# Cross-attention on one core: value and denominator products joined, reciprocals on query lanes, row maxima started two steps earlier

## The reference

```python
def _L0_xattn_ref(target, source, target_mask, source_mask, Wq, bq, Wk, bk, Wv, bv):
    ...
    dot = jnp.einsum('bhdt,bhds->bhts', q, k) / math.sqrt(HEAD_DIM)
    mask = target_mask[:, :, :, None] * source_mask[:, :, None, :]
    dot = mask * dot - (1.0 - mask) * NEG
    amap = jax.nn.softmax(dot, axis=-1) * mask
    out = jnp.einsum('bhts,bhds->bhdt', amap, v)
    return out.reshape(b, HEADS * HEAD_DIM, t)
```

## Time and profile before

| | us |
|---|---|
| median of 3 runs | 4644.87 (4640.8 to 4647.98) |
| the profiled execution, its own time | 4640.3 |
| its span (first to last instruction) | 4638.4 |
| PE / DVE / ACT / POOL busy in the span | 4277.3 / 3240.8 / 2228.5 / 569.1 |
| cross-attention, first load to last addition to x | 3178.2 to 3987.6 |

### The profile page before, as it was taken

The page is one execution under the profiler, slowest core; times in us unless marked ns, Lnnn a source line. Parts: engine busy times, 40 slices in busy tenths (PEclk is TensorE's granted clock), DMA queues, the critical chain, the costliest instruction groups (busy, mean ns, idle before and its releaser), DMA issues. The chain is left out here.

```text
span 4638.4 us, 79836 instructions
## 1 busy us (share of the span) xinstructions
PE 4277.3 (92%) x28448; PEld 3104.3 (67%) x28448; DVE 3240.8 (70%) x6458; ACT 2228.5 (48%) x4055; POOL 569.1 (12%) x540
## 2 busy tenths in 40 slices
PE   3999999999999999999999999995998999479998
PEld 2777777777777777777777777773333333168887
DVE  3788888888888888888888888884555556532222
ACT  1555556565555555565555555551444444321111
POOL 1010011000110001101010011001232222311110
PEclk8999999999999999999999999996899899789999
DMA  2000000000000000000000000003444444000000
GB/s 70 1 17 13 11 15 13 13 10 11 15 15 11 10 11 16 15 11 15 11 16 10 11 15 15 6 1 65 82 88 77 79 79 73 38 23 19 19 14 37
DMA packets 67490, 124.28 MB, mean 27 GB/s; under 512 B 10460, under 2 KB 12380, under 8 KB 66556
## 3 DMA queue, kind: packets, MB, share of 16 engines
q1 hardware_dynamic: 64636, 117.79, 11.6%
q10 hardware_dynamic: 2432, 1.05, 0.1%
HBM read 95.14 MB, written 21.50 MB: 25 GB/s over the span
## 5 line engine op out<-in xcount | busy, mean ns | idle before, releaser
L387 PE MATMUL pj<-xh,w_hi 128*128 128x512 f32 x1536 | 688.8, 448 | 30.5 <-ACT conv_k L618 15.9
L387 PE MATMUL pj<-xh,w_lo 128*128 128x512 f32 x1536 | 609.0, 396 | 0.0
L387 PE MATMUL pj<-xl,w_hi 128*128 128x512 f32 x1536 | 603.5, 393 | 0.0
L1473 DVE TENSOR_REDUCE row_max<-s 128x1 f32<-128x512 f32 x512 | 339.5, 682 | 309.0 <-PE s L1255 307.6
L1409 ACT ACTIVATE probs<-s 128x512 f32<-128x512 f32 x512 | 288.7, 596 | 344.5 <-PE s L1276 263.2
L387 PEld LDWEIGHTS pj<-xh,w_hi 128*128 128x128 f32 x1536 | 291.5, 190 | 79.9 <-issue 31.1
L387 PEld LDWEIGHTS pj<-xh,w_lo 128*128 128x128 f32 x1536 | 289.6, 189 | 67.5
L689 ACT ACTIVATE kk_masked<-tp 128x512 f16<-128x512 f32 x320 | 191.4, 598 | 291.2 <-PE tp L493 287.9
L998 POOL CAST w_hi<-w_raw 128x512 fp32r<-128x512 f32 x96 | 73.7, 768 | 2083.7 <-PE pj L387 2079.2
L387 PEld LDWEIGHTS pj<-xl,w_hi 128*128 128x128 f32 x1536 | 293.1, 191 | 50.3 <-issue 14.8
L758 DVE SCALAR_TENSOR_TENSOR conv_v<-conv_in,conv_w_section,conv_v 128x512 f32<-128x512 f32 x384 | 296.6, 772 | 8.0 <-ACT conv_v L618 3.4
(11 more groups left out here) (266 smaller groups left out, 10496.9 us busy)
## 6 DMA issues: line engine op xcount, KB each, us to landing
w_raw<-in_w_in SPq DMA_DIRECT2D x128, 256.0 KB, 2.6
q_stack<-qk_parts SPq DMA_DIRECT2D x128, 128.0 KB
k_stack<-qk_parts SPq DMA_DIRECT2D x128, 128.0 KB
f_raw<-in_f_w SPq DMA_DIRECT2D x32, 256.0 KB, 2.6
x_all<-in_x SPq DMA_DIRECT2D x4, 1024.0 KB, 9.4
source<-in_ctx SPq DMA_DIRECT2D x8, 512.0 KB
qk_parts<-q_hi SPq DMA_DIRECT2D x16, 256.0 KB, 2.0
qk_parts<-q_lo SPq DMA_DIRECT2D x16, 256.0 KB, 2.0
```

Source lines behind the costliest of these rows:

```text
L387: mm = pe.matmul(pj[j % 2][:, :], a[:, j, k * P:(k + 1) * P], b[:, k, bp * WIN:(bp + 1) * WIN], start=(n == 0), stop=(n == 3 * KT - 1))
L1473: dve.reduce_max(mx[g % 2][:, i:i + 1], s1[n % 2][:, :], AX_X).then_inc(E["rm"].sem, 1)
```

## The change

All of it is in `cross_attention`:

1. The 16 spare columns of each head's 32 value weights are set to 1, so that one product gives numerators and denominators. The heads of even e go to bank `av[0]`, those of odd e to `av[1]`; `pe_denominators` as a pass over the probabilities is gone, 8 sets of 4 products per unit.
2. ACT copies `av[0]` at step 20 of the same unit and `av[1]` at step 4 of the next. PE picks the denominators out by 8 float32 products with 128x128 weights and 4 moving columns (steps 8 to 11), so that queries are on the partitions; DVE takes one reciprocal of 128x32 (step 12); POOL spreads and masks it; PE turns it back with 4 products of 128x128 (steps 18 to 21); DVE multiplies (step 24).
3. POOL joins the two copies (`pool_mix`: two products with a column of 0 and 1, one addition) ahead of the low part of the queries, and does one final addition where it had three operations.
4. LEAD is 28. The steps of the transposition, rounding, write and read back of the maxima are 5 steps apart from write to read, and their DRAM buffer is doubled, each half with its own semaphore.
5. The stacks have 128 rows; the rows between the masks and the maxima are zeroed at the start by POOL and ACT, and SP waits for that before its next transfers.
6. SP's program is written out: in an even unit the stack of the next unit comes first and the load of context and mask after it. `mask_final` is gone.

```diff
-LEAD = 26
+LEAD = 28
 STEPS, SETS = 4 * HH, HH
-R_MASK, R_MAX, K_ROWS = 4 * XD, 4 * XD + 4, 4 * XD + 6
+R_MASK, R_MAX, K_ROWS = 4 * XD, P - 2, P
...
-        av_n, av_d = m.ps("av_num"), m.ps("av_den")
+        av = [m.ps(f"av{e}") for e in range(2)]
...
+            sp.wait_ge(blank, 2)
+            sp.wait_ge(blank_odd, 2)
...
+            start()
+            for u in range(UNITS):
+                b, f = u // 2, u % 2
+                if u < UNITS - 1:
+                    stack(u + 1, 1 - f, 1, u - 1 if u else None)
+                    stack_masks((u + 1) // 2, 1 - f, 1)
+                if u < UNITS - 2:
+                    if f == 0:
+                        load(b + 1, False)
+                    parts(u + 2, f, 0)
+                    parts(u + 2, f, 1)
+                    stack(u + 2, f, 0, u)
+                    stack_masks(b + 1, f, 0)
...
+            if not isinstance(keys_before, int) or keys_before >= 3:
+                E["o"].wait(pe, keys_before - 3, 0)
...
-        def pe_numerators(pe, u, f, k):
+        def pe_values(pe, u, f, k):
             e, st = k // 4, k % 4
             if k == 0:
                 E["vz"].wait(pe, u, 1)
-                if not is_first(u):
-                    E["oc"].wait(pe, u - 1, 0)
+            if st == 0 and not is_first(u):
+                E["oc"].wait(pe, u - 1, e)
             E["ex"].wait(pe, u, 4 * k + 3)
             for j in range(QD):
-                mm = pe.matmul(av_n[32 * j:32 * j + 32, :], vz[f][:, st, 2 * j + e, :], pt[:, (4 * k + j) % RP, :],
-                               start=(k == 0), stop=(k == SETS - 1))
-            mm.then_inc(E["avn"].sem, 1)
-        def pe_denominators(pe, u, k):
-            if k == 0 and not is_first(u):
-                E["oc"].wait(pe, u - 1, 1)
-            for j in range(QD):
-                mm = pe.matmul(av_d[32 * j:32 * j + 32, :], dz[:, k // 4, :], pt[:, (4 * k + j) % RP, :],
-                               start=(k == 0), stop=(k == SETS - 1))
+                mm = pe.matmul(av[e][32 * j:32 * j + 32, :], vz[f][:, st, 2 * j + e, :], pt[:, (4 * k + j) % RP, :],
+                               start=(st == 0), stop=(st == 3))
             mm.then_inc(E["av"].sem, 1)
+        def pe_denominators(pe, u, t):
+            if t == 0:
+                E["oc"].wait(pe, u, 1)
+            for e in range(2):
+                c = 16 * (1 - e)
+                mm = pe.matmul(turn[:, 2 * P + t * HH + e:2 * P + (t + 1) * HH:2], nb[e][:, t * P:(t + 1) * P],
+                               cols["ident"][:, c:P:32], start=(t == 0 and e == 0), stop=(t == 3 and e == 1),
+                               skip_group_check=True)
+            if t == 3:
+                mm.then_inc(E["dt"].sem, 1)
+        def pe_spread(pe, u, t):
+            if t == 0:
+                E["rt"].wait(pe, u, 0)
+            mm = pe.matmul(pb[:, t * P:(t + 1) * P], rt[:, t, :, :].rearrange("p h d -> p (h d)"), cols["ident"],
+                           start=(t == 0), stop=(t == 3), skip_group_check=True)
+            if t == 3:
+                mm.then_inc(E["rx"].sem, 1)
...
                 k = n // 4 - 1
                 if n % 4 == 1 and k >= 0:
-                    pe_numerators(pe, u, f, k)
+                    pe_values(pe, u, f, k)
                 elif n % 4 == 1 and not is_first(u):
-                    pe_numerators(pe, u - 1, 1 - f, SETS - 1)
-                if n % 4 == 3 and k >= 0:
-                    pe_denominators(pe, u, k)
-                elif n % 4 == 3 and not is_first(u):
-                    pe_denominators(pe, u - 1, SETS - 1)
+                    pe_values(pe, u - 1, 1 - f, SETS - 1)
                 if n == 1 and has1:
                     pe_source_values(pe, 1 - f, u + 1)
                 if n == 9 and has2:
                     pe_queries(pe, u + 2, b + 1, f)
                 if n == 12 and has2:
                     pe_keys(pe, u + 2, b + 1, f)
-                if n == 7:
+                if 8 <= n < 12 and not is_first(u):
+                    if n == 8:
+                        E["mxl"].wait(pe, u, 3)
+                    pe_denominators(pe, u - 1, n - 8)
+                if 18 <= n < 22 and not is_first(u):
+                    if n == 18 and has2:
+                        E["full"].wait(pe, u + 2, 1)
+                    elif n == 18 and has1:
+                        E["vsb"].wait(pe, u + 1, 0)
+                    pe_spread(pe, u - 1, n - 18)
+                if n == 5:
                     pe_turn_max(pe, u, 3)
-                elif n in (15, 23, 31) and has1:
+                elif n in (13, 21, 29) and has1:
...
-            if g == 0:
-                E["mr"].wait_before(act, u)
+            if g >= 2:
+                E[f"mr{g % 2}"].wait(act, u, 15)
             else:
-                E["mr"].wait(act, u, 16 * g - 1)
+                E[f"mr{g % 2}"].wait_before(act, u)
             for i, part in enumerate((mxh, mxl)):
-                act.dma_start(max_d[i], part[:, :].bitcast(F32)).then_inc(E["mw"].sem, 16)
+                act.dma_start(max_d[g % 2, i], part[:, :].bitcast(F32)).then_inc(E["mw"].sem, 16)
...
-        def act_out(act, u):
-            E["av"].wait(act, u, SETS - 1)
-            E["x"].wait_before(act, u)
-            act.activation(num[:, :], av_n[:, :], ACT.Copy).then_inc(E["oc"].sem, 1)
-            act.activation(den[:, :], av_d[:, :], ACT.Copy).then_inc(E["oc"].sem, 1)
+                          max_d[g % 2].rearrange("o (h q) t -> o h (q t)", h=2)).then_inc(E[f"mr{g % 2}"].sem, 16)
+        def act_out(act, u, e):
+            E["av"].wait(act, u, 4 * e + 3)
+            E["dt"].wait_before(act, u)
+            E["mix"].wait_before(act, u)
+            act.activation(nb[e][:, :], av[e][:, :], ACT.Copy).then_inc(E["oc"].sem, 1)
...
-                    act_out(act, u - 1)
+                    act_out(act, u - 1, 1)
+                if n == 20:
+                    act_out(act, u, 0)
...
-                if n == 2:
-                    act_max_out(act, u, 2)
+                if n == 4:
+                    act_max_in(act, u, f, 2)
                 elif n == 5:
-                    act_max_in(act, u, f, 2)
+                    act_max(act, u, 3)
                 elif n == 7:
-                    act_max(act, u, 3)
-                elif n == 9:
                     act_max_out(act, u, 3)
                 elif n == 12:
                     act_max_in(act, u, f, 3)
+                elif n in (13, 21, 29) and has1:
+                    act_max(act, u + 1, n // 8 - 1)
                 elif n in (15, 23, 31) and has1:
-                    act_max(act, u + 1, n // 8 - 1)
-                elif n in (17, 25) and has1:
-                    act_max_out(act, u + 1, n // 8 - 2)
+                    act_max_out(act, u + 1, n // 8 - 1)
                 elif n in (20, 28) and has1:
...
-        def dve_recip(dve, u, i):
-            if i == 0:
-                E["oc"].wait(dve, u, 1)
-                E["x"].wait_before(dve, u)
-            sl = slice(i * P, (i + 1) * P)
-            dve.reciprocal(rd[:, sl], den[:, sl]).then_inc(E["rd"].sem, 1)
+        def dve_recip(dve, u):
+            E["dt"].wait(dve, u, 0)
+            E["rt"].wait_before(dve, u)
+            dve.reciprocal(rc[:, :, :], turn[:, 2 * P:2 * P + 4 * HH].rearrange("p (t h) -> p t h", h=HH)).then_inc(E["rc"].sem, 1)
+        def dve_out(dve, u):
+            E["rx"].wait(dve, u, 0)
+            E["mix"].wait(dve, u, 2)
+            dve.tensor_tensor(rd[:, :], nm[:, :], pb[:, :], ALU.mult).then_inc(E["o"].sem, 1)
...
-                if 6 <= n <= 9 and not is_first(u):
-                    dve_recip(dve, u - 1, n - 6)
+                if n == 12 and not is_first(u):
+                    dve_recip(dve, u - 1)
+                if n == 24 and not is_first(u):
+                    dve_out(dve, u - 1)
...
+        def pool_mix(pool, u):
+            E["oc"].wait(pool, u, 1)
+            E["o"].wait_before(pool, u)
+            pool.tensor_scalar(nm[:, :], nb[0][:, :], half[:, 0:1], None, ALU.mult).then_inc(E["mix"].sem, 1)
+            E["x"].wait_before(pool, u)
+            pool.tensor_scalar(rd[:, :], nb[1][:, :], half[:, 1:2], None, ALU.mult).then_inc(E["mix"].sem, 1)
+            E["mix"].wait(pool, u, 1)
+            pool.tensor_tensor(nm[:, :], nm[:, :], rd[:, :], ALU.add).then_inc(E["mix"].sem, 1)
+        def pool_recip(pool, u):
+            E["rc"].wait(pool, u, 0)
+            E["rx"].wait_before(pool, u)
+            pool.tensor_tensor(rt[:, :, :, :], rc[:, :, :].unsqueeze(3).to_broadcast([P, 4, HH, XD]),
+                               mcol[:, u // 2, :].unsqueeze(2).unsqueeze(3).to_broadcast([P, 4, HH, XD]), ALU.mult)                .then_inc(E["rt"].sem, 1)
...
+            for t in (qs[0], ks[0]):
+                pool.memset(t[R_MASK:, :, :].bitcast(F32), 0.0).then_inc(blank, 1)
+            pool.wait_ge(blank, 2)
             for f in range(2):
-                pool.memset(vz[f][:, :, :, :], 0.0).then_inc(zeroed, 1)
```

(71 more changed lines are left out.)

61 lines of the change are left out of this document (32 added, 29 removed).

## The result

| | before | after |
|---|---|---|
| median of the runs, us | 4646.42 (4640.8 to 4651.64) | 4614.74 (4612.91 to 4616.41) |
| ratio, 95% interval | | 0.9931 (0.9916 to 0.9947) |
| span of the profiled execution, us | 4638.4 | 4612.0 |

The direction was right, the size was not: 4614.74 us lies above the range of 4488 to 4612. It is nearest to the rival in which the waits for the maxima stay (4606 us, chance 0.24), with a start that cost more on top.

The account below looks back on a forecast made before the run. PE sets the pace at 47.9 us a unit, 39.7 without idle time and low clock. 39.7 - 9.6 + 1.9 + 3.9 = 35.9; with stalls odd 37.8, even 45.5; with start and end -86.5, 4558 us, range 4488 to 4612.

Parts of the forecast that it names:

- the rival in which the waits for the maxima stay: Stack transfers cover more of each unit, one more stall per unit costs 3.4 us: 4606 us, chance 0.24.
- The work in a unit: A unit without stalls falls from 39.7 to 35.9 us.
- The added products: On PE, the pick-out costs 2.5 us and the turn back 1.4, sum +3.9 us a unit, bounds 2.0 and 5.6.
- The product taken out: One of two column products per four PE steps goes, -9.6 us a unit; DVE's round trip takes back 1.9.
- four steps of the plain kind: PE alone needs 3.04 us for four steps; waiting for DVE's reductions with two pass-1 banks makes it 3.41.
- Maxima with 5 steps: Five steps, about 4.6 us, from write to read against landings of 2.9 to 5.0; 0.9 idle, 1.0 low clock a unit.
- SP's order: In even units the load behind the stack makes DVE idle 5 us, PE about 5.8: 9.6 us per even unit.
- Start and end: Zeroing delays SP's load at the start by 7.3 us; the longer chain at the end adds 0.5: +7.8 us.
- The clock: Scores on 128 rows may bring PE's clock back earlier, counted as one third of each long low-clock spell.

Follow-up runs that it names:

- the direct transfers: The change with the maxima's parts moved straight to the score stack, without DRAM write and read back: 4589.7 us, ratio 0.9878.
- four edits: The change with maxima moved straight to the stack, load before second half stack, pass 1 waiting two steps back, first load before zeroing wait: 4546.33 us, 0.9800.

## Why the prediction was wrong, step by step

- **The work in a unit: right, in part by luck.** 35.52 us against 35.9, from 39.76 against 39.7. Two terms erred against each other. The added products cost 2.0 us, not 3.9: a pick-out slot takes 0.36 us (3582.60 to 3582.96 in PE's timeline), four of them 1.4, and the turn back 0.15 a slot. The score behind each slot is followed by the next 0.08 to 0.09 us later than elsewhere; with these it is 2.7. (The 1.7 us that the prediction puts inside its bounds is the pick-out's alone; the bounds are the sum's.) The product taken out frees 6.2 to 6.9 (4.24 and the 2.0 to 2.7), not 7.7; four steps of the plain kind take 3.54 us, not 3.41.
- **"Maxima with 5 steps": the step that failed.** It left 0.9 us idle and 1.0 of low clock a unit. The odd unit shown idles 5.1 us and loses about 2.5 to the clock (0.94 of 42.83). The step took the landing for a duration, 2.9 to 5.0 us, that more steps would cover. It is a date: the end of the half stack ahead. As the unit got shorter and the write was issued earlier, it moved closer to the stack's start and waited longer. The two numbers came from one unit and were read too narrowly: at 3612.77 ACT had not been waiting for the landing, so 2.9 is only a bound from above, and the same trace has landings up to 7.1 us at step 5, where PE idled too, so that its idle stretches were not only the two of the earlier trace rows. Nor was the stack read to its end: its packets ran to 3591, 11.1 us behind the first issue, not 9.2. Odd units miss the forecast by 7 x 4.3 us and even ones, which idle 2.4 and 0.5 us at step 28 for the same reason, by 7 x 2.7: about the 49.8 us missed in the 14 units (87.5 forecast, 37.7 measured), of which 14 belong to the wait for all 32 maxima below. Of the rest the direct transfers gave back 17, with idle time of their own behind the four issues. That the remainder is the landing too is argued from the timelines, not shown by a run. The rival's text had it, with the reason that the work shrinks and the bytes do not.
- **"SP's order": right in kind, a little high.** DVE idled 3.81 us (forecast 5), PE 4.55 (5.8) in the unit shown. But the step named only the even units' cost. Putting the load back gave 29 us, 19 in the units and 10 at the start.
- **The wait for all 32 maxima: overlooked.** 1.02 us a unit; the prediction moved the lead to 28 and did not name what then stands ahead of the last maxima on DVE.
- **"Start and end": half.** The source values come 6.6 us later (7.3 forecast; 1.3 of it lies ahead of the stage, where SP's first issue is later too). The first pass-2 score comes 14.7 later. SP no longer holds the next half stack back until the load may go, so it floods the engines just before the maxima's read back. The load first took most of that away. The rest, the last two units and the tail, gave 3.5 instead of 6.3 us.
- **The clock: small.** A third of each spell was counted for filled rows; removing them cost 19 us by the ratios in the change (11 by the medians), though it spared 7 at the start.

Of the 60 us between forecast (-86.5) and profile (-26.4), 49.8 are units, 7.4 start, 2.8 end. With the waits removed and the rest of the change kept, four edits gave 2.0%, 93 us.

## What to carry to other kernels

When a small transfer must land while bulk transfers are queued, give it a place ahead of them or nothing to wait on it; more steps only help up to the end of the bulk. The wait at step 5 went when its write was moved to the bulk's first issue, and ACT waited again, for less, when it was issued two steps later. When a change shortens the loop, recompute every transfer's landing from what is issued ahead of it, since that time does not shrink. And a wait removed must be followed to the buffer behind it: here it reappeared at step 0, then on ACT's single buffer, and only the second buffer turned it into time.

## What the runs showed of the hardware that was not expected

A write of 4 KB on ACT's queue took at most 2.9 us in a quiet moment, and 4.8, 5.0 or 7.8 us beside SP's stack, by how much of its 1.1 MB was issued ahead and still to move; a small transfer behind a whole half stack was through 12.6 to 13.4 us from the stack's first issue in five kernels. A product with 128 columns of weights and only 4 moving columns took 0.09 us a pass (16 in 1.4 us), or 0.11 with the delay behind it, beside 0.13 with 128. Each direct transfer of the maxima held ACT for about 0.6 us (two in 1.19; the writes to DRAM had 0.28 and 0.32), and four in a row made PE idle 1.0 to 1.2.
